# Two halves counted apart, and row indices made at arrival, in the routed-expert stage of a transformer layer kernel

## The chip, the cores and the metric

The kernel runs on one core of a Trainium2 chip. Its time is the device time of one execution in microseconds, taken as the median of several runs. TensorE (PE) does the matrix products; VectorE (DVE) and ScalarE (ACT) do elementwise work and copy out of PSUM; GpSimd (POOL) issues the indirect DMAs; SyncE (SP) and ACT issue the direct ones. All engines work beside each other and order themselves by semaphores. A DMA adds 16 to its semaphore when it has landed.

## The reference

x has 64 sequences of 64 tokens with 256 features, 4096 tokens in all. The reference adds two things to it.

```python
x = x + attention1(moe8_top2(x))             # 8 experts, 2 of them a token, and a shared one
x = x + ffn(attention2(x))                   # layernorm, shared key and value, causal, layernorm
# ffn: xf (4096 x 256)
tidx, tw = route(xf)                         # 64 experts, 8 a token, weights normed and scaled by 2.5
for e in experts:                            # up_w[e]: 256 x 128, down_w[e]: 128 x 256
    acc += combine[:, e, None] * (relu(xf @ up_w[e]) ** 2 @ down_w[e])
out = acc + shared(xf)
```

The change touches the loop over the 64 routed experts and nothing else.

## The kernel before

Ahead of the last stage the kernel has written, for each pair of a token and one of its 8 experts, a row of 258 numbers into a DRAM table `x_slots`: the token's 256 features, a number from which the pair's row in the result table is made (entry D), and the routing weight (entry D + 1). The table is sorted by expert and padded to blocks of 128 slots with one expert each: 320 blocks. Slots that hold no pair get an index past the end, and a scatter leaves them out.

The last stage is `slot_experts` (L1827). It takes the blocks in 80 groups of four (`GB = 4`). A group's work is spread over three turns of a software pipeline, and the five engines each run the same sequence of turns (`pipeline`, L1870): turn n does step 0 of group n, step 1 of group n - 1 and step 2 of group n - 2. `w` is n modulo 4.

- Step 0. SP loads the group's 512 slot rows to `xs` (L1900), in one of two buffers, as soon as DVE's `t_dve` tells that the group two before has been copied. PE transposes them (L1934) once the rows have landed and ACT and DVE have copied the transposes of the group before. ACT copies half of the transposes to `xsT` (L1981), DVE the other half (L2031); ahead of it DVE copies index number and weight of each row to `tail` (L2030), a ring of four (`TR`). ACT also copies the four experts' up weights to `up` (L1978).
- Step 1. PE makes z, the up products (L1945); ACT makes relu(z) (L1986) and DVE multiplies it by max(z, 0) into `hT` (L2036).
- Step 2. PE makes y, the down products of the four blocks (L1957), in two PSUM banks, 4 and 5. One count, `y_ps`, tells that all four are there. ACT scales blocks 0 and 1 by the routing weight into `ys` (L1992), DVE makes the row indices `yidx` from `tail` (L2044) and scales blocks 2 and 3 (L2047). Then POOL, after waiting for both, issues four indirect DMAs (L1914), one a block, that scatter the rows of `ys` to the DRAM table `y_rows`, a row for each pair.

`ys` and `yidx` have two buffers. So ACT and DVE wait, ahead of step 2, until the scatters of the group two before have landed; one semaphore of each buffer counts all four (`y_out[w % 2]`). In a turn, each engine does step 0 first, then step 1, then step 2, in the order of the program. PE waits for both ACT's and DVE's outputs of the group before ahead of its y products.

From turn 28 on (`HOLD`) there is a fourth kind of work. A tile of 128 tokens has all of its rows in `y_rows` by then. In each turn ACT issues the gather of half a tile's rows (512 KB, L2005), after its step 2, and DVE adds them up in three additions (L2056, L2060, L2065) at the end of the next turn. ACT stores a finished tile to `out` every second turn. Ahead of a tile's first gather ACT waits until all scatters up to some groups back have landed. After group 79 the rest of the 64 halves is gathered and added with nothing beside it.

Nothing in this stage is ordered by a planner: the order of the instructions on each engine is that of the code in `turn`.

Of the kernel before, what the change touches and what calls it, by code (L numbers as in the profile page):

```python
# [15 lines left out]
P = 128  # L16
# [29 lines left out]
GB = 4  # L46
# [67 lines left out]
def build(nc, x, xT, condT, cond, bias2, mask, w1gate, w1up, w1down, wtT, wgT,  # L114
# [3 lines left out]
    with ctx:  # L118
# [1708 lines left out]
        def slot_experts():  # L1827
# [4 lines left out]
            with ph:  # L1832
# [3 lines left out]
                def sem(name):  # L1836
# [23 lines left out]
                t_ps, t_act, t_dve, up_ready, z_ps, r_ready, h_ready, y_ps, y_act, y_dve = (  # L1860
                    sem(n) for n in ("t_ps", "t_act", "t_dve", "up_ready", "z_ps", "r_ready", "h_ready",
                                     "y_ps", "y_act", "y_dve"))
                block = ph.enter_context(nc.Block())
                LAG = 2

# [39 lines left out]
                @block.gpsimd  # L1905
                def _(pool):
                    def turn(n, w, q, live, u):
                        if live(2):
                            g = n - 2
                            pool.wait_ge(y_act, g + 1)  # L1910
                            pool.wait_ge(y_dve, g + 1)
                            pool.nop(nofuse=True)
                            for b in range(GB):
                                pool.indirect_dma_start(  # L1914
                                    out=y_rows, out_offset=bass.IndirectOffsetOnAxis(ap=yidx[:, w % 2, b:b + 1], axis=0),
                                    in_=ys[:, w % 2, b, :], in_offset=None,
                                    bounds_check=T * K2 - 1, oob_is_err=False).then_inc(y_out[w % 2], 16)
                    pipeline(pool, turn)
                    for w in range(2):
                        pool.wait_ge(y_out[w], NG // 2 * 16 * GB)  # L1920

                @block.tensor
                def _(pe):
# [3 lines left out]
                    def turn(n, w, q, live, u):  # L1927
# [20 lines left out]
                        if live(2):  # L1948
                            g = n - 2
                            e = experts_of(pe, regs, g)  # L1950
                            pe.wait_ge(h_ready, g + 1)
                            if isinstance(g, int) and g == 0:
                                pe.wait_ge(wd_in, (-(-EARLY // WCOLS) - (EARLY - E2) // WCOLS) * 16)
                            wait(pe, y_act, g)
                            wait(pe, y_dve, g)
                            for b in range(GB):
                                last = pe.matmul(ps[:, 4 + b // 2, (b % 2) * D:(b % 2 + 1) * D],  # L1957
                                                 hT[:, w % 2, b, :],
                                                 w_dn[:, bass.ds(e[b], 1), :].rearrange("p o n -> p (o n)"),
                                                 start=True, stop=True)  # L1960
                            last.then_inc(y_ps, 1)
                    pipeline(pe, turn)

                @block.scalar
                def _(act):
# [6 lines left out]
                    def turn(n, w, q, live, u):  # L1972
# [9 lines left out]
                        if live(1):  # L1982
                            g = n - 1
                            act.wait_ge(z_ps, g + 1)
                            wait(act, y_ps, g - 1)
                            act.activation(hT[:, (w - 1) % 2].rearrange("p b m -> p (b m)"), ps[:, 2, :], ACT.Relu).then_inc(r_ready, 1)  # L1986
                        if live(2):
                            g = n - 2
                            act.wait_ge(y_ps, g + 1)
                            wait(act, y_out[w % 2], half(q, w, 2) * 16 * GB)  # L1990
                            for b in range(2):
                                last = act.activation(ys[:, w % 2, b, :], ps[:, 4, b * D:(b + 1) * D], ACT.Copy,  # L1992
                                                      scale=tail[:, (w - 2) % TR, b, 1:2])
                            last.then_inc(y_act, 1)
                        if u is not None and not (isinstance(u, int) and u >= HALVES):
                            act.nop(nofuse=True)
                            tile = q * 2 + w // 2 - HOLD // 2
                            if w == 0:
                                done = q * 2 - 2 if not isinstance(q, int) else min(q * 2 - 2, NG // 2)
                                for sent in y_out:  # L2000
                                    act.wait_ge(sent, done * 16 * GB)
# [20 lines left out]
                def _(dve):  # L2022
                    def turn(n, w, q, live, u):
                        if live(0):
                            dve.wait_ge(t_ps, n + 1)
                            wait(dve, z_ps, n - 1)
                            wait(dve, y_act, n - TR + 1)
                            wait(dve, y_dve, n - TR + 1)
                            dve.nop(nofuse=True)
                            dve.tensor_copy(tail[:, w], xs[:, w % XR, :, D:D + 2])  # L2030
                            dve.tensor_copy(xsT[:, w % 2, 2:4].rearrange("p b c m -> p (b c m)"), ps[:, 1, :]  # L2031
                                            ).then_inc(t_dve, 1)
                        if live(1):
# [4 lines left out]
                                                     ).then_inc(h_ready, 1)  # L2038
                        if live(2):
                            g = n - 2  # L2040
                            dve.wait_ge(y_ps, g + 1)
                            wait(dve, y_out[w % 2], half(q, w, 2) * 16 * GB)

                            dve.tensor_scalar(yidx[:, w % 2, :], tail[:, (w - 2) % TR, :, 0], -1.0, float(T * K2),  # L2044
                                              ALU.mult, ALU.add)
                            for b in range(2, GB):
                                last = dve.tensor_scalar(ys[:, w % 2, b, :], ps[:, 5, (b - 2) * D:(b - 1) * D],  # L2047
                                                         tail[:, (w - 2) % TR, b, 1:2], None, ALU.mult)
# [100 lines left out]
```

## Time and profile before

| | us |
|---|---|
| median of 3 runs | 1892.97 |
| lowest and highest | 1887.82, 1893.12 |
| the profiled execution | 1889.07 |
| its span, first to last instruction | 1887.3 |
| POOL's scatters of this stage (L1914) | 323.3 busy, 320 of them |
| gathers of a half tile (L2005) | 64, 5.0 to landing |

The profile is of one execution. Its page gives each engine's busy time, the span in 40 slices, the chain of work that ended last followed back from the end, and groups of instructions. Times of single instructions come from the trace of the same execution, and are counted from the span's start. The stage of the change lies between some 1384 us, when its first slot rows are on their way, and the end. A POOL row of a scatter shows the time in which POOL makes the transfer's descriptors, not the transfer. Busy PE time is modelled at its end.

### The profile page before, as it was taken

Reading aid. Unit: us, or ns where it says so; the run is one execution under the profiler, and the core shown is the slowest. Engines: PE = TensorE matmul, PEld = TensorE weight load, DVE = VectorE, ACT = ScalarE, POOL = GpSimd, SP = SyncE. Lnnn points to the kernel's source line nnn. Section 1 sums busy time; section 2 is a strip of 40 time slices with the busy share of each in tenths; the row PEclk is TensorE's granted clock in tenths of the full one; section 3 lists DMA queues with packets and bytes.
Section 4 is the critical chain, followed back from the end, with each engine's and each line's share of the span. In section 5 each row is a group of like instructions: output and inputs, shape, how many; then the busy total and the mean of one; then the engine's idle time right before and its main releaser. Section 6 shows DMA issues by size and latency. Waiting matters only on the chain. (4 is left out here: it accounts for less than half of the span.)

```text
span 1887.3 us, 35739 instructions
## 1 busy us (share of the span) xinstructions
PE 1552.3 (82%) x12092; PEld 1241.4 (66%) x12093; DVE 1238.6 (66%) x3320; ACT 824.3 (44%) x1581; POOL 1000.5 (53%) x869
## 2 busy tenths in 40 slices
PE   5699999988888869989998898987039888888880
PEld 2588888854655547777776777755038886777770
DVE  2677776746767655688878888797214446666674
ACT  2233333223444434555555555544025555555550
POOL 1233333336665432226565566667717776766772
PEclk9899999999998989999999999998559999999996
DMA  5278458012000000001111111117646678988975
GB/s 151 64 187 230 116 137 232 1 31 57 24 24 13 13 23 2 1 1 57 57 49 55 57 55 59 49 63 280 189 175 191 194 208 271 284 280 260 280 218 166
DMA packets 155436, 226.61 MB, mean 120 GB/s; under 512 B 28840, under 2 KB 127791, under 8 KB 153140
## 3 DMA queue, kind: packets, MB, share of 16 engines
q1 hardware_dynamic: 113124, 115.37, 21.9%
q0 software_dynamic: 27648, 67.44, 10.1%
q10 hardware_dynamic: 14544, 42.21, 7.0%
q8 instruction: 75, 1.23, 0.3%
q14 instruction: 45, 0.37, 0.1%
HBM read 110.57 MB, written 122.75 MB: 124 GB/s over the span
## 5 line engine op out<-in xcount | busy, mean ns | idle before, releaser
L1914 POOL DMA_INDIRECT y_rows<-se_ys,se_yidx x320 | 323.3, 1010 | 158.3 <-issue 96.6
L1106 POOL DMA_INDIRECT x_slots<-wide,a_sidx x256 | 251.2, 981 | 71.6 <-issue 71.1
L442 POOL TENSOR_TENSOR e_hl<-e_h,e_hh 128x512 fp32r<-128x512 f32 x80 | 103.6, 1295 | 228.9 <-ACT e_hh L426 228.9
L1095 POOL TENSOR_TENSOR flat<-flat,a_rs 128x512 f32<-128x512 f32 x64 | 67.4, 1053 | 234.2 <-DVE a_rs L1582 234.2
L1957 PE MATMUL ps<-wide,se_hT 128*128 x640 | 157.4, 389 | 26.6 <-DVE se_ys L2047 26.2
L1934 PE MATMUL ps<-ident,se_xs 128*128 128x128 f32 x640 | 89.2, 285 | 101.4 <-DMA se_xs<-x_slots 80.1
L1945 PE MATMUL ps<-se_xsT,se_up 128*128 128x128 f32 x1280 | 163.0, 281 | 5.4 <-DVE se_hT L2036 3.9
L1945 PEld LDWEIGHTS ps<-se_xsT,se_up 128*128 128x128 f32 x1280 | 152.4, 195 | 13.6 <-issue 8.1
L1934 PEld LDWEIGHTS ps<-ident,se_xs 128*128 128x128 f32 x640 | 75.1, 147 | 123.2 <-issue 81.4
L1978 ACT COPY se_up<-w_up 128x256 f32 x320 | 105.8, 402 | 99.8 <-issue 86.4
L1957 PEld LDWEIGHTS ps<-wide,se_hT 128*128 128x128 f32 x640 | 116.6, 192 | 46.3 <-issue 33.3
L374 PE MATMUL ps<-xh,wh 128*128 128x512 f32 x320 | 126.7, 396 | 15.2 <-PEq L189 15.2
L461 DVE SCALAR_TENSOR_TENSOR acc<-ps,e_cexp,acc 128x256 f32<-128x256 f32 x320 | 132.2, 476 | 1.0 <-PE ps L376 0.6
L1992 ACT ACTIVATE se_ys<-ps,se_tail 128x256 f32<-128x256 f32 x160 | 67.2, 471 | 139.4 <-DMA y_rows<-se_ys,se_yidx 132.6
L1216 PE MATMUL ps<-w_up 128*128 128x256 f32 x448 | 114.5, 404 | 14.5 <-DVE flat L1675 8.8
L375 PE MATMUL ps<-xl,wh 128*128 128x512 f32 x320 | 126.4, 395 | 0.0
L1176 PE MATMUL ps<-w_up,flat 128*128 128x256 f32 x512 | 120.2, 389 | 6.8 <-ACT flat L1352 6.8
L376 PE MATMUL ps<-xh,wl 128*128 128x512 f32 x320 | 125.4, 392 | 0.0
L469 DVE TENSOR_TENSOR e_r<-ps,e_r 128x512 f32<-128x512 f32 x80 | 55.3, 692 | 98.5 <-ACT e_r L423 98.5
L1176 PEld LDWEIGHTS ps<-w_up,flat 128*128 128x128 f32 x512 | 98.8, 195 | 29.2 <-ACT flat L1352 9.5
L579 POOL TENSOR_TENSOR flat<-flat,a_mx 128x1024 f32<-128x1024 f32 x32 | 60.9, 1903 | 93.2 <-DVE a_mx L801 93.2
L2036 DVE SCALAR_TENSOR_TENSOR se_hT<-ps,se_hT 128x512 f32<-128x512 f32 x80 | 55.3, 692 | 81.9 <-ACT se_hT L1986 81.3
(277 smaller groups left out, 3812.9 us busy)
## 6 DMA issues: line engine op xcount, KB each, us to landing
x_slots<-wide SPq DMA_DIRECT2D x40, 1032.0 KB, 14.4
se_xs<-x_slots SPq DMA_DIRECT2D x80, 516.0 KB
se_got<-y_rows ACTq DMA_DIRECT2D x64, 512.0 KB, 5.0
w_up<-in_up SPq DMA_DIRECT2D x8, 1024.0 KB, 16.9
y_rows<-se_ys,se_yidx POOLq DMA_INDIRECT x320
wide<-in_xT SPq DMA_DIRECT2D x2, 2048.0 KB, 10.3
flat<-in_x SPq DMA_DIRECT2D x8, 512.0 KB, 3.9
x_slots<-wide,a_sidx POOLq DMA_INDIRECT x256, 2.9
```

What stands on the lines that cost most here:

```text
L374: pe.matmul(out, h0, h1, start=start, stop=False)
L375: pe.matmul(out, h0, l1, start=False, stop=False)
L376: return pe.matmul(out, l0, h1, start=False, stop=stop)
L461: last = dve.scalar_tensor_tensor(acc[:, tile, :], y_bank(n, t), cexp[:, w, tile:tile + 1], acc[:, tile, :], ALU.mult, ALU.add)
L1106: pool.indirect_dma_start(out=x_slots, out_offset=bass.IndirectOffsetOnAxis(ap=sidx[:, t, k_:k_ + 1], axis=0), in_=stage[:, t, k_, :], in_ ...
L1176: last = pe.matmul(ps[:, 1, 0:D], oT[:, j, :], wo[:, j, :], start=(j == 0), stop=(j == J2 - 1))
L1216: last = pe.matmul(bank[:, a * 2 * P:(a + 1) * 2 * P], wq[:, c, (2 * jj + a) * P:(2 * jj + a + 1) * P], xT_[:, c, u * 2 * P:(u + 1) * 2 * ...
L1914: pool.indirect_dma_start(out=y_rows, out_offset=bass.IndirectOffsetOnAxis(ap=yidx[:, w % 2, b:b + 1], axis=0), in_=ys[:, w % 2, b, :], in ...
L1934: last = pe.transpose(ps[:, b // 2, (b % 2 * C + c) * P:(b % 2 * C + c + 1) * P], xs[:, w % XR, b, c * P:(c + 1) * P], ident[:])
L1945: last = pe.matmul(ps[:, 2, b * P:(b + 1) * P], up[:, (w - 1) % 2, b, c, :], xsT[:, (w - 1) % 2, b, c, :], start=(c == 0), stop=(c == C - 1))
L1957: last = pe.matmul(ps[:, 4 + b // 2, (b % 2) * D:(b % 2 + 1) * D], hT[:, w % 2, b, :], w_dn[:, bass.ds(e[b], 1), :].rearrange("p o n -> p ...
L1978: last = act.copy(up[:, w % 2, b], w_up[:, bass.ds(e[b], 1)].rearrange("p o c m -> p (o c) m"))
```

## The change

Step 2's two halves get counts of their own. `y_ps` becomes `ya_ps` (blocks 0 and 1, PSUM bank 4, ACT) and `yb_ps` (blocks 2 and 3, bank 5, DVE). `y_out` gets one semaphore for each buffer and half. PE waits for ACT's half of the group before ahead of its first two products, and for DVE's ahead of the other two. POOL issues the first half's scatters after `y_act` alone, then waits for `y_dve` and issues the others. ACT, ahead of its half, waits for the first half's scatters of the group two before; DVE for the second half's.

`yidx` becomes a ring of four and is made in step 0, straight from `xs`, ahead of the copies to `tail` and `xsT`; `tail` now holds the weight alone. As POOL's scatters read the indices, DVE waits in step 0 of turn n until both halves of group n - 4 have landed. POOL waits for `t_dve` too, which tells that the indices are there.

```diff
-                yidx = sb("yidx", [P, 2, GB], I32)
-                tail = sb("tail", [P, TR, GB, 2])
+                yidx = sb("yidx", [P, TR, GB], I32)
+                tail = sb("tail", [P, TR, GB])
...
-                y_out = [sem("y_out0"), sem("y_out1")]
+                y_out = [[sem("y_out0a"), sem("y_out0b")], [sem("y_out1a"), sem("y_out1b")]]
...
 # POOL, step 2
-                            pool.wait_ge(y_act, g + 1)
-                            pool.wait_ge(y_dve, g + 1)
-                            pool.nop(nofuse=True)
-                            for b in range(GB):
-                                pool.indirect_dma_start(
-                                    out=y_rows, out_offset=bass.IndirectOffsetOnAxis(ap=yidx[:, w % 2, b:b + 1], axis=0),
-                                    in_=ys[:, w % 2, b, :], in_offset=None,
-                                    bounds_check=T * K2 - 1, oob_is_err=False).then_inc(y_out[w % 2], 16)
+                            pool.wait_ge(t_dve, g + 1)
+                            for side, done in enumerate((y_act, y_dve)):
+                                pool.wait_ge(done, g + 1)
+                                pool.nop(nofuse=True)
+                                for b in range(2 * side, 2 * side + 2):
+                                    pool.indirect_dma_start(
+                                        out=y_rows,
+                                        out_offset=bass.IndirectOffsetOnAxis(ap=yidx[:, (w - 2) % TR, b:b + 1], axis=0),
+                                        in_=ys[:, w % 2, b, :], in_offset=None,
+                                        bounds_check=T * K2 - 1, oob_is_err=False).then_inc(y_out[w % 2][side], 16)
...
 # PE, step 2
-                            wait(pe, y_act, g)
-                            wait(pe, y_dve, g)
-                            for b in range(GB):
-                                last = pe.matmul(ps[:, 4 + b // 2, (b % 2) * D:(b % 2 + 1) * D],
...
-                            last.then_inc(y_ps, 1)
+                            for side, (free_, full) in enumerate(((y_act, ya_ps), (y_dve, yb_ps))):
+                                wait(pe, free_, g)
+                                for b in range(2 * side, 2 * side + 2):
+                                    last = pe.matmul(ps[:, 4 + side, (b % 2) * D:(b % 2 + 1) * D],
...
+                                last.then_inc(full, 1)
...
 # ACT, step 1, then step 2
-                            wait(act, y_ps, g - 1)
+                            wait(act, yb_ps, g - 1)
...
-                            act.wait_ge(y_ps, g + 1)
-                            wait(act, y_out[w % 2], half(q, w, 2) * 16 * GB)
+                            act.wait_ge(ya_ps, g + 1)
+                            wait(act, y_out[w % 2][0], half(q, w, 2) * 32)
...
 # DVE, step 0
+                            wait(dve, y_out[w % 2][0], half(q, w, 2) * 32)
+                            wait(dve, y_out[w % 2][1], half(q, w, 2) * 32)
                             dve.nop(nofuse=True)
-                            dve.tensor_copy(tail[:, w], xs[:, w % XR, :, D:D + 2])
+                            dve.tensor_scalar(yidx[:, w, :], xs[:, w % XR, :, D], -1.0, float(T * K2), ALU.mult, ALU.add)
+                            dve.tensor_copy(tail[:, w, :], xs[:, w % XR, :, D + 1])
                             dve.tensor_copy(xsT[:, w % 2, 2:4].rearrange("p b c m -> p (b c m)"), ps[:, 1, :]
                                             ).then_inc(t_dve, 1)
...
 # DVE, step 2
-                            dve.wait_ge(y_ps, g + 1)
-                            wait(dve, y_out[w % 2], half(q, w, 2) * 16 * GB)
-
-                            dve.tensor_scalar(yidx[:, w % 2, :], tail[:, (w - 2) % TR, :, 0], -1.0, float(T * K2),
-                                              ALU.mult, ALU.add)
+                            dve.wait_ge(yb_ps, g + 1)
+                            wait(dve, y_out[w % 2][1], half(q, w, 2) * 32)
+                            dve.nop(nofuse=True)
```

ACT's wait ahead of a tile's first gather goes over the four semaphores in place of two, with the same groups in it.

## Rows read from the trace of the kernel before

**Rows 1.** The page's slices: busy tenths of the DMA engines, 40 equal parts.
```profile
DMA  5278458012000000001111111117646678988975
```
**Rows 2.** The page's chain that ended last, share of the span.
```profile
DMA y_rows<-se_ys,se_yidx 7%; POOL y_rows L1914 5%; DMA se_got<-y_rows 1%; PE ps L1945 1%; DVE se_ys L2047 1%; PE ps L1957 1%; DMA se_xs<-x_slots 1%; PE ps L1934 1%; ACT se_up L1978 0%; ACT se_hT L1986 0%; DVE se_yidx L2044 0%; POOLq L1914 0%; DVE se_got L2056 0%; ACT se_xsT L1981 0%; ACTq L1867 0%
```
**Rows 3.** Busy by stretch: length, busy (count), PEclk, DMA share, GB/s; L1914, then all engines.
```profile
1411.80:1552.00 140.20, 105.21 (x107) 0.99 0.63 192
1552.00:1832.00 280.00, 197.92 (x194) 0.98 0.87 270
...
1552.00:1838.00 286.00, 243.75 (x1585) 207.39 (x1583) 187.81 (x450) 156.97 (x400) 202.68 (x199) 0.98 0.86 267
```
**Rows 4.** Waits after 1360 us: total, times, longest.
```profile
ACT se_ys L1992 <- DMA y_rows<-se_ys,se_yidx: 132.6, 68, 5.5
...
DVE se_yidx L2044 <- DMA y_rows<-se_ys,se_yidx: 84.1, 57, 4.7
...
PE ps L1934 <- DMA se_xs<-x_slots: 80.1, 7, 73.6
```
**Rows 5.** The chain in order of time: start, length; from a last scatter's start to landing.
```profile
1443.07 3.95 DMA y_rows<-se_ys,se_yidx
...
1515.51 5.45 DMA y_rows<-se_ys,se_yidx
...
1662.16 5.59 DMA y_rows<-se_ys,se_yidx
...
1673.67 5.80 DMA y_rows<-se_ys,se_yidx
```
**Rows 6.** POOL's scatters in order of time: start, length, idle time before.
```profile
1669.62 1.16 POOL L1914 DMA_INDIRECT y_rows<-se_ys,se_yidx  x1 [0.82 <-DVE se_ys L2047]
1671.09 0.99 POOL L1914 DMA_INDIRECT y_rows<-se_ys,se_yidx  x1 [0.30 <-issue]
...
1673.67 0.99 POOL L1914 DMA_INDIRECT y_rows<-se_ys,se_yidx  x1 [0.30 <-issue]
```
**Rows 7.** DVE in order of time.
```profile
1667.85 0.17 DVE L2044 TENSOR_SCALAR se_yidx<-se_tail 128x4 int32<-128x4 f32 x1 [0.58 <-DMA y_rows<-se_ys,se_yidx]
1667.93 0.87 DVE L2047 TENSOR_SCALAR se_ys<-ps,se_tail 128x256 f32<-128x256 f32 x2
...
1811.64 0.68 DVE L2031 COPY se_xsT<-ps 128x512 f32<-128x512 f32 x1
1812.63 0.69 DVE L2036 SCALAR_TENSOR_TENSOR se_hT<-ps,se_hT 128x512 f32<-128x512 f32 x1 [0.31 <-ACT se_hT L1986]
```
**Rows 8.** PE in order of time.
```profile
1677.76 1.06 PE L1934 MATMUL ps<-ident,se_xs 128*128 128x128 f32 x8 [1.38 <-DMA se_xs<-x_slots]
...
1691.12 1.94 PE L1934 MATMUL ps<-ident,se_xs 128*128 128x128 f32 x8 [2.91 <-DMA se_xs<-x_slots]
...
1812.47 1.06 PE L1934 MATMUL ps<-ident,se_xs 128*128 128x128 f32 x8 [0.34 <-DVE se_xsT L2031]
1813.47 2.02 PE L1945 MATMUL ps<-se_xsT,se_up 128*128 128x128 f32 x16
1815.33 1.89 PE L1957 MATMUL ps<-wide,se_hT 128*128 x8
1817.11 1.09 PE L1934 MATMUL ps<-ident,se_xs 128*128 128x128 f32 x8
```
**Rows 9.** DVE's copies that let the rows of 1677.76 and 1691.12 be loaded.
```profile
1670.54 0.69 DVE L2031 COPY se_xsT<-ps 128x512 f32<-128x512 f32 x1
...
1682.60 0.68 DVE L2031 COPY se_xsT<-ps 128x512 f32<-128x512 f32 x1
```
**Rows 10.** ACT after a landing, its gather's issue, and gathers on the page.
```profile
1802.25 0.84 ACT L1992 ACTIVATE se_ys<-ps,se_tail 128x256 f32<-128x256 f32 x2 [0.93 <-DMA y_rows<-se_ys,se_yidx]
1802.70 0.34 ACTq L2005 DMA_DIRECT2D se_got<-y_rows  x1
...
se_got<-y_rows ACTq DMA_DIRECT2D x64, 512.0 KB, 5.0
```

More of the change, by code:

```diff
@@ L1909, in turn @@
                             g = n - 2
-                            pool.wait_ge(y_act, g + 1)
-                            pool.wait_ge(y_dve, g + 1)
-                            pool.nop(nofuse=True)
-                            for b in range(GB):
-                                pool.indirect_dma_start(
-                                    out=y_rows, out_offset=bass.IndirectOffsetOnAxis(ap=yidx[:, w % 2, b:b + 1], axis=0),
-                                    in_=ys[:, w % 2, b, :], in_offset=None,
-                                    bounds_check=T * K2 - 1, oob_is_err=False).then_inc(y_out[w % 2], 16)
+                            pool.wait_ge(t_dve, g + 1)
[8 more added lines that the diff above has]
+                                        bounds_check=T * K2 - 1, oob_is_err=False).then_inc(y_out[w % 2][side], 16)
                     pipeline(pool, turn)
                     for w in range(2):
-                        pool.wait_ge(y_out[w], NG // 2 * 16 * GB)
+                        for side in range(2):
+                            pool.wait_ge(y_out[w][side], NG // 2 * 32)
                 @block.tensor
@@ L1953, in turn @@
                                 pe.wait_ge(wd_in, (-(-EARLY // WCOLS) - (EARLY - E2) // WCOLS) * 16)
-                            wait(pe, y_act, g)
-                            wait(pe, y_dve, g)
-                            for b in range(GB):
-                                last = pe.matmul(ps[:, 4 + b // 2, (b % 2) * D:(b % 2 + 1) * D],
-                                                 hT[:, w % 2, b, :],
-                                                 w_dn[:, bass.ds(e[b], 1), :].rearrange("p o n -> p (o n)"),
-                                                 start=True, stop=True)
-                            last.then_inc(y_ps, 1)
+                            for side, (free_, full) in enumerate(((y_act, ya_ps), (y_dve, yb_ps))):
+                                wait(pe, free_, g)
+                                for b in range(2 * side, 2 * side + 2):
+                                    last = pe.matmul(ps[:, 4 + side, (b % 2) * D:(b % 2 + 1) * D],
+                                                     hT[:, w % 2, b, :],
+                                                     w_dn[:, bass.ds(e[b], 1), :].rearrange("p o n -> p (o n)"),
+                                                     start=True, stop=True)
+                                last.then_inc(full, 1)
                     pipeline(pe, turn)
@@ L1988, in turn @@
                             g = n - 2
-                            act.wait_ge(y_ps, g + 1)
-                            wait(act, y_out[w % 2], half(q, w, 2) * 16 * GB)
+                            act.wait_ge(ya_ps, g + 1)
+                            wait(act, y_out[w % 2][0], half(q, w, 2) * 32)
                             for b in range(2):
                                 last = act.activation(ys[:, w % 2, b, :], ps[:, 4, b * D:(b + 1) * D], ACT.Copy,
-                                                      scale=tail[:, (w - 2) % TR, b, 1:2])
+                                                      scale=tail[:, (w - 2) % TR, b:b + 1])
                             last.then_inc(y_act, 1)
@@ L1999, in turn @@
                                 done = q * 2 - 2 if not isinstance(q, int) else min(q * 2 - 2, NG // 2)
-                                for sent in y_out:
-                                    act.wait_ge(sent, done * 16 * GB)
+                                for sent in y_out[0] + y_out[1]:
+                                    act.wait_ge(sent, done * 32)
                                     act.nop(nofuse=True)
@@ L2040, in turn @@
                             g = n - 2
[L2041 to L2045 removed]
+                            dve.wait_ge(yb_ps, g + 1)
+                            wait(dve, y_out[w % 2][1], half(q, w, 2) * 32)
+                            dve.nop(nofuse=True)
                             for b in range(2, GB):
                                 last = dve.tensor_scalar(ys[:, w % 2, b, :], ps[:, 5, (b - 2) * D:(b - 1) * D],
[L2048 removed]
+                                                         tail[:, (w - 2) % TR, b:b + 1], None, ALU.mult)
                             last.then_inc(y_dve, 1)
```

4 lines of the change are left out of this document (2 added, 2 removed).

## Prediction

> **What bounds the kernel now.** I read the page's slices first, then the chain of waits, then POOL's scatters by stretch, then single turns. The last stage runs from slice 30 on, and the DMA engines stand at 7 to 9 tenths in it [rows 1]; in its longest stretch POOL is busy 197.92 of 280 us and DVE 187.81 of 286 [rows 3], so neither is plainly full. The chain's longest piece is the landing of the y scatters, then their issue on POOL [rows 2]. So the stage hangs on POOL and on what POOL waits for.
>
> Rows 3 split it. Between 1411.8 and 1552 us POOL issues 107 scatters in 140.2 us: 1.31 us each. Back to back one takes 1.29 us (0.99 plus a pause of 0.30: 1671.09 [rows 6]), so there POOL is full: 5.17 us for a group of four. Between 1552 and 1832, with the gathers running, 194 scatters take 280 us: 1.443 each, 5.77 a group. At 1.29 they would take 250.3 us. What can be won in that stretch is at most 29.7 us, and about 2 in the first.
>
> Why 5.77: ACT and DVE wait for the landing of the group two before, because one count holds all four scatters of a buffer; they wait 132.6 and 84.1 us [rows 4]. One ring of two groups: last scatter issued to landing 5.7 us (5.59, 5.80 [rows 5]); indices 0.08 (1667.85 to 1667.93) and both products 0.87 [rows 7]; 0.82 until POOL starts (1668.80 to 1669.62); first to last scatter 4.05 (1669.62 to 1673.67 [rows 6]). Sum 11.52, 5.76 a group: the measured 5.77. In the first stretch landing took 3.95 [rows 5]: 9.8 for two, under POOL's 10.34, and POOL rules.
>
> **The change, part by part.** Work is nearly unchanged: the same 4 products, 4 scatters, one index operation of 0.17 and one tail copy (half as wide) per group. Cost 0; DVE is idle a third of the stretch [rows 3]. POOL gets one wait and one nop more. Where POOL is late, its first scatter takes 1.16, not 0.99 [rows 6]. If both halves are late, that is 0.17 x 48.5 groups = 8 us; if not, 0, as a group's border costs nothing when POOL isn't late. I take 0: the second half has the 2.6 us of the first half's scatters as cover.
>
> *Halves apart.* ACT's half is free when the first two scatters of the old group have landed, 2 x 1.29 = 2.6 us before the last. It needs only the first half of the product. The old ring shrinks: ACT's side no longer waits for the last landing. For DVE's side the ring ends with two scatters, not four: 5.7 + DVE's work + 0.82 + 1.29.
>
> *Indices at arrival.* This is where something is added. DVE now waits at the head of turn n for both halves of group n-4 (the ring of four index slots), before the indices, the tail and the copy of xT(n). The same landing was awaited before, at the turn's end, behind xT(n) and hT(n-1). Behind the waiting instruction now stand: xT(n), which lets SP load the slot rows of n+2 and PE transpose n+1; hT(n-1), which lets PE run product z(n); DVE's half of y(n-2); and the gather's additions. From landing: 0.08 for the indices, as much for the tail, 0.68 for xT: 0.84 to its end (1811.64), hT 0.69, y 0.87 [rows 7]: 2.4 to 2.6 before POOL can have the second half. New rings:
> - DVE's half, 2 groups: 5.7 + 2.5 + 0.82 + 1.29 = 10.3, 5.16 a group: level with POOL.
> - Through the transposes, 3 groups: 5.7 + 0.84 + 0.15 to PE (1812.32 to 1812.47) + transposes 1.00 + z 1.86 + half a y product 1.0 [rows 8] + ACT's half 0.9 (0.84 [rows 10] and a hand-over) + 0.82 + 4.05 = 16.3, 5.44 a group.
> - Through the load of slot rows, 4 groups: landing n-4, xT(n), load of n+2, transposes, z(n+1), y(n), scatters of n: 5.7 + 0.84 + X + 3.86 + 0.9 + 0.82 + 4.05 = 16.17 + X. X is DVE's copy to the rows' arrival. No row gives it as such. Below: 1817.11 minus 1812.32, 4.8 us, no wait for rows. Above: 1677.76 minus 1671.23, 6.5, and 1691.12 minus 1683.28, 7.8, where PE did wait [rows 8, 9]; beside the first, of 73.6 us, there were six such waits in the stage, 6.5 us together [rows 4]. X = 4.8, 6.5, 7.8 give 5.24, 5.67, 5.99 a group. I take 6.0, nearer to 6.5 since the rows' load is then bunched behind the landing: 22.2 / 4 = 5.54.
>
> Second stretch: the longest ring, 5.54, 0.23 below 5.77, times 48.5 groups: -11 us (at X = 4.8 the three-group ring takes over, 5.44 and -16; at X = 7.8 it is +11). First stretch: with 3.95 to 5.45 landing [rows 5], say 4.5, the rings are 15.1 / 3 = 5.03 and (14.97 + 6.0) / 4 = 5.24 against POOL's 5.17: 0, at most +2, at best -2. The start gains under 1 us, as POOL may begin with ACT's half. The tail of gathers alone after the last scatter is untouched, and for the few scatters after 1832 I count nothing.
>
> Sum: span 1887.3 - 11 = 1876; the profiled execution took 1889.07 beside that span, so 1878; the median of the runs shown, 1892.97, stands 3.9 above it: 1882.
>
> **A rule weighed.** The row shows a DMA share of 0.87 in the gathering stretch, 0.63 before it, and landings of 3.95 in the one and 5.8 in the other [rows 3, 5]. The Trainium skill, page "DMA: Bandwidth & Descriptors", section "Queues, rings and completion order", says that each DMA engine takes turns between the queues that have work for it. By it a load that starts together with a gather would get half the engines' turns; the trace's longer landings agree. This is the third rival's mechanism.
>
> **The rivals.** A difference under 0.3% (5.7 us) is what a measurement here can't tell from none.
> 1. POOL full throughout (chance 0.12): landing and X stay short, everything hides behind 1.29 x 4. 28 to 30 us less: 1864. For: POOL and both landings were level in the first stretch. Against: the three-group ring of 5.44, and the DMA share would go to 0.87 x 5.77 / 5.17 = 0.97.
> 2. One wait replaces the other (0.25): X near 6.9 gives 23.1 / 4 = 5.77; or the share goes up and landings with it (by 5.77 / 5.54 x 0.87 = 0.91 for my forecast). 0 to -4: 1891. For: 6.5 was seen with the load spread out. Against: 4.8 was seen too, in the same stretch.
> 3. Slower (0.18): the load of slot rows and the gather meet. Now ACT sends the gather 0.45 us after the landing (1802.70, the landing at 1802.25) and the load goes 3.4 us after it (1667.85 to 1671.23 [rows 7, 9]); both carry some 512 KB, and a gather takes 5.0 us [rows 10]. By my ring the load goes 0.84 after the landing; ACT's half of n ends 0.84 + 6.0 + 3.86 + 0.9 = 11.6 after it, so that of n-2, ahead of the gather in turn n, ends 11.6 - 2 x 5.54 = 0.5 after it: both leave within 0.4 us. If X passes 6.9, the turn is longer than before; at 7.4 it is 23.57 / 4 = 5.89, +6 us, and the first stretch, where X is not hidden any more either, adds up to +2: 1899 to 1901. For: 7.8 was seen once. Against: the scatters between them are spread better, and gathers tolerate a late landing (DVE takes them 2.3 us or more after).
> That the change doesn't do what it says I rule out: the counts and the waits are plain in the diff.
>
> **How the numbers follow.** Forecast 0.45 (5.45 to 5.65 a group, -15 to -6: 1878 to 1887), rivals 0.12, 0.25, 0.18. Faster by over 0.3% (under 1887.3): rival 1 and nearly all of the forecast, 0.12 + 0.43 = 0.55. Within: 0.02 of the forecast and 0.24 of rival 2, 0.26. Slower (over 1898.6): rival 3 and 0.01 of rival 2, for POOL's 0.17 us restarts, 0.19. The range holds the forecast, rival 2, most of rival 3's lower end and rival 1's upper: 1866 to 1899.
>
> **What would show it.** In the profile after: ACT's waits for y_rows nearly gone, replaced by waits for PE's y product; DVE's wait for y_rows standing before the index operation at the head of the turn, in the size of 80 us or more; PE's transposes waiting for se_xs and for DVE's copy, tens of us instead of the 6.5 for rows; 194 scatters in about 269 us of the gathering stretch. If POOL shows no pauses beyond 0.30, rival 1 holds; if the transposes wait over 1 us for rows in most turns, rival 2 or 3. Wrong would be: a first stretch longer by more than 3 us, or ACT still waiting for landings.

## The result, and the profile after

The changed kernel took 1905.32 us (median of 20 runs, 1888.38 to 1912.65) against 1892.95 for the one before (20 runs, 1887.82 to 1900.34): ratio 1.0066, 95% interval 1.0051 to 1.0081. The forecast was 1882 and faster; it is slower, by 12.4 us. The profiled execution took 1911.96 us, near the top of its range, with a span of 1910.2 (before: 1889.07 and 1887.3), so the trace shows nearly twice the loss of the medians: 22.9 us against 12.4.

POOL's scatters by stretch, as in [rows 3]: length, busy (count), granted clock, DMA share, GB/s; changed kernel.

```profile
1411.80:1552.00 140.20, 106.41 (x108) 1.00 0.64 192
1552.00:1832.00 280.00, 177.97 (x178) 0.89 0.82 254
```

The first stretch is as it was (108 scatters, 107 before). In the gathering stretch there are 178 in 280 us in place of 194: 6.29 us a group in place of 5.77. That is nearly the whole loss (the last scatter starts at 1879.20 us in place of 1857.01), and the granted clock there went from 0.98 to 0.89. Who waited, as in [rows 4]: total, times, longest.

```profile
PE ps L1937 <- DMA se_xs<-x_slots: 81.5, 6, 73.6
PE ps L1937 <- DVE se_xsT L2037: 68.6, 34, 4.2
...
DVE se_yidx L2035 <- DMA y_rows<-se_ys,se_yidx: 128.8, 45, 5.0
...
ACT se_ys L1995 <- PE ps L1960: 22.2, 66, 1.4
ACT se_ys L1995 <- DMA y_rows<-se_ys,se_yidx: 2.6, 1, 2.6
```

ACT's 132.6 us of waiting for landings are down to 2.6, as the change meant. DVE's went from 84.1 to 128.8, at the head of the turn, and behind them PE's transposes wait 68.6 us for DVE's copy (6.2 before). For slot rows PE waits 7.9 us beside the first wait, in five turns that all lie between 1584 and 1616 us: the load that I feared binds there and nowhere after.

One round of the ring, in order of time: start, length, idle time before. It is the three-group ring of the prediction.

```profile
1691.09 0.17 DVE L2035 TENSOR_SCALAR se_yidx<-se_xs 128x4 int32<-128x4 f32 x1 [4.98 <-DMA y_rows<-se_ys,se_yidx]
...
1691.24 0.68 DVE L2037 COPY se_xsT<-ps 128x512 f32<-128x512 f32 x1
...
1692.07 1.94 PE L1937 MATMUL ps<-ident,se_xs 128*128 128x128 f32 x8 [4.24 <-DVE se_xsT L2037]
...
1693.80 3.55 PE L1948 MATMUL ps<-se_xsT,se_up 128*128 128x128 f32 x16
...
1697.19 1.89 PE L1960 MATMUL ps<-wide,se_hT 128*128 x8
...
1698.35 0.84 ACT L1995 ACTIVATE se_ys<-ps,se_tail 128x256 f32<-128x256 f32 x2 [0.28 <-PE ps L1960]
...
1700.03 0.98 POOL L1915 DMA_INDIRECT y_rows<-se_ys,se_yidx  x1 [3.44 <-issue]
...
1703.89 0.98 POOL L1915 DMA_INDIRECT y_rows<-se_ys,se_yidx  x1 [0.30 <-issue]
...
1710.58 0.17 DVE L2035 TENSOR_SCALAR se_yidx<-se_xs 128x4 int32<-128x4 f32 x1 [4.32 <-DMA y_rows<-se_ys,se_yidx]
```

Landing seen to DVE's copy done 0.83, to PE 0.15, start of the transposes to start of y 5.12, to ACT 1.16, ACT 0.84, to POOL 0.84, first to last scatter 3.86, to the landing 6.69: 19.49 us for three groups. The forecast for the same steps was 16.3. Two terms make the difference: transposes and z take 5.12 in place of 2.86 (+2.26), and the landing 6.69 in place of 5.7 (+0.99). The first comes with the clock. After PE has stood 4.24 us the transposes take 1.94 us and z 3.55; in the next turn they take 1.04 and 1.95. After a shorter pause the clock holds:

```profile
1590.58 1.06 PE L1937 MATMUL ps<-ident,se_xs 128*128 128x128 f32 x8 [1.92 <-DVE se_xsT L2037]
1591.48 1.95 PE L1948 MATMUL ps<-se_xsT,se_up 128*128 128x128 f32 x16
1593.27 1.89 PE L1960 MATMUL ps<-wide,se_hT 128*128 x8
```

The length of the pause alone doesn't decide it. After pauses of 3.88 and 4.02 us (1767.50 and 1805.01) the transposes still ran at full speed and only the z products behind them were slow:

```profile
1767.50 1.06 PE L1937 MATMUL ps<-ident,se_xs 128*128 128x128 f32 x8 [3.88 <-DVE se_xsT L2037]
1768.40 3.21 PE L1948 MATMUL ps<-se_xsT,se_up 128*128 128x128 f32 x16
```

The granted clock in the round shown, behind the pause and in the turn after it (length, busy of PE, PEld, DVE, ACT and POOL, then clock, DMA share, GB/s):

```profile
1692.10:1696.90 4.80, 4.80 (x23) 4.80 (x24) 3.53 (x9) 0.59 (x1) 2.47 (x3) 0.50 0.60 180
1698.90:1703.30 4.40, 4.40 (x33) 4.14 (x32) 3.50 (x9) 2.91 (x9) 2.67 (x3) 1.00 0.81 270
```

This round is one of the longer ones. From DVE's wait at 1632.70 to that at 1839.19 the ring goes round eleven times without a break, in 18.77 us on the mean: 4.52 from the start of the transposes to the start of y (3.87 to 5.15), and landings of 6.46. Against the forecast's 2.86 and 5.7 that is 1.66 us for the first and 0.76 for the second.

So the ring lengthens itself: waiting for one landing in three turns, PE falls to the lower of its two clocks (0.50 of full speed, 1.2 GHz), and comes late to the next. The Trainium skill, page "TensorE: Matmul & The Clock Gate", section "Part 1: The HAM clock gate", says that a monitor lets the array run at full or at half clock by how busy PE has been of late. The rows agree: 1.94 over 1.04 and 3.55 over 1.95 are 1.87 and 1.82, near a factor of two.

### The profile page after: what moved, and what is told of

It is laid out like the page before. It is cut to its first block and busy times, and to the rows that moved or that the text cites. A ratio compares the mean times of both kernels' runs of the same rounds, so it can differ in the third digit from the quotient of the medians.

```text
span 1910.2 us, 35964 instructions
## 1 busy us (share of the span) xinstructions
PE 1556.2 (81%) x12092; PEld 1262.7 (66%) x12093; DVE 1236.7 (65%) x3320; ACT 831.2 (44%) x1581; POOL 994.9 (52%) x869
## 5 line engine op out<-in xcount | busy, mean ns | idle before, releaser
L1915 POOL DMA_INDIRECT y_rows<-se_ys,se_yidx x320 | 318.7, 996 | 185.5 <-issue 136.1
L1937 PE MATMUL ps<-ident,se_xs 128*128 128x128 f32 x640 | 96.1, 300 | 150.5 <-DMA se_xs<-x_slots 81.5
L1937 PEld LDWEIGHTS ps<-ident,se_xs 128*128 128x128 f32 x640 | 80.5, 155 | 170.6 <-issue 167.5
L1948 PE MATMUL ps<-se_xsT,se_up 128*128 128x128 f32 x1280 | 177.2, 299 | 0.2 <-DVE se_hT L2042 0.2
L1948 PEld LDWEIGHTS ps<-se_xsT,se_up 128*128 128x128 f32 x1280 | 171.2, 216 | 0.6 <-issue 0.4
L1960 PE MATMUL ps<-wide,se_hT 128*128 x640 | 153.4, 384 | 0.3 <-ACT se_ys L1995 0.3
L2035 DVE TENSOR_SCALAR se_yidx<-se_xs 128x4 int32<-128x4 f32 x80 | 18.0, 225 | 209.5 <-DMA y_rows<-se_ys,se_yidx 128.8
L1216 PEld LDWEIGHTS ps<-w_up 128*128 128x128 f32 x448 | 85.2, 198 | 34.2 <-DVE flat L1675 11.2
```

The source lines that it names most:

```text
L1216: last = pe.matmul(bank[:, a * 2 * P:(a + 1) * 2 * P], wq[:, c, (2 * jj + a) * P:(2 * jj + a + 1) * P], xT_[:, c, u * 2 * P:(u + 1) * 2 * ...
L1915: pool.indirect_dma_start(out=y_rows, out_offset=bass.IndirectOffsetOnAxis(ap=yidx[:, (w - 2) % TR, b:b + 1], axis=0), in_=ys[:, w % 2, b, ...
L1937: last = pe.transpose(ps[:, b // 2, (b % 2 * C + c) * P:(b % 2 * C + c + 1) * P], xs[:, w % XR, b, c * P:(c + 1) * P], ident[:])
L1948: last = pe.matmul(ps[:, 2, b * P:(b + 1) * P], up[:, (w - 1) % 2, b, c, :], xsT[:, (w - 1) % 2, b, c, :], start=(c == 0), stop=(c == C - 1))
L1960: last = pe.matmul(ps[:, 4 + side, (b % 2) * D:(b % 2 + 1) * D], hT[:, w % 2, b, :], w_dn[:, bass.ds(e[b], 1), :].rearrange("p o n -> p (o ...
```

## The experiments

Ten kernels ran, some of them several times, in five groups and eighteen runs. In the first and the last group the kernel before took 1893 us. In the three between it took 2035 to 2052 us, once on the very chip of the first group, and the ratios of those three are compared with each other alone.

### 1 and 2. Each part by itself

Halves apart alone (e1_halves_only): the changed kernel, with

```diff
 # POOL, step 2
-                            pool.wait_ge(t_dve, g + 1)
+                            pool.wait_ge(idx_ready, g + 1)
...
 # DVE, step 0
-                            wait(dve, y_out[w % 2][0], half(q, w, 2) * 32)
-                            wait(dve, y_out[w % 2][1], half(q, w, 2) * 32)
...
-                            dve.tensor_scalar(yidx[:, w, :], xs[:, w % XR, :, D], ...)
...
 # DVE, step 2, from a two-column tail, ring of four
+                            wait(dve, y_out[w % 2][0], (half(q, w, 2) - 1) * 32)
+                            wait(dve, y_out[w % 2][1], (half(q, w, 2) - 1) * 32)
...
+                            dve.tensor_scalar(yidx[:, (w - 2) % TR, :], tail[:, (w - 2) % TR, :, 0], ...).then_inc(idx_ready, 1)
```

> The changed kernel with one part undone: row indices are made in step 2 again (from a two-column tail, in a ring of four, with a count of their own), so VectorE no longer waits for a landing at the head of its turn; the two halves stay apart. Theory A (the wait at the head, in the ring landing - VectorE's copy - transposes - z - y - scatters, is what makes the change slow): that ring is gone, POOL goes from 6.3 us a group to 5.2 to 5.5 in the gathering stretch, the granted clock there is back at 0.97 or more, and the kernel beats the one before: 1865 to 1885. Theory B (the halves apart are what is slow: POOL waits twice, the scatters come in longer clumps and land later): it stays above the one before, 1898 to 1910, with landings of 6.5 us and more.

Measured: 1886.35 us, ratio 0.9965 (0.9948 to 0.9983).

Indices at arrival alone (e2_early_only): the kernel before, with

```diff
+                            wait(dve, y_out[w % 2], half(q, w, 2) * 16 * GB)   # step 0
...
+                            dve.tensor_scalar(yidx[:, w, :], xs[:, w % XR, :, D], ...)
...
-                            dve.tensor_scalar(yidx[:, w % 2, :], tail[:, (w - 2) % TR, :, 0], ...)   # step 2
```

> The kernel before with the other part alone: indices made at arrival in a ring of four, with VectorE's wait for the landing of group n-4 at the head of turn n; the four scatters of a group and both products still counted together. Theory A: now both the head wait and the old ring stand: VectorE's half comes 2.5 us after a landing in place of 0.95, before all four scatters, 5.7 + 2.5 + 0.8 + 4.05 = 13.1 for two groups, 6.5 a group against 5.77: slower than before by 30 to 45 us, 1922 to 1940. Theory B: about the time of before, 1888 to 1898.

Measured: 1944.09 us, ratio 1.0276 (1.0259 to 1.0293). POOL's scatters by stretch in e2:

```profile
1411.80:1552.00 140.20, 98.67 (x101) 1.00 0.58 174
1552.00:1832.00 280.00, 173.61 (x171) 0.93 0.79 244
```

and DVE's wait for landings in it:

```profile
DVE se_yidx L2031 <- DMA y_rows<-se_ys,se_yidx: 203.5, 68, 4.7
```

171 scatters in 280 us are 6.55 us a group; 6.5 was written down. DVE's waits for landings are 203.5 us. The wait at the head of the turn is what costs: 2.76% on top of the old ring, and 1.0% on top of the halves (1.0066 against 0.9965). The halves are what pays: theory B falls. The sizes of e1 were missed by theory A all the same. The halves alone gain 0.35%, not the 0.4% to 1.5% that were expected, and the gathering stretch runs at the old pace. POOL's scatters in the stretch, in e1:

```profile
1552.00:1832.00 280.00, 193.01 (x194) 0.92 0.85 267
```

PE's waits for slot rows in e1:

```profile
PE ps L1938 <- DMA se_xs<-x_slots: 114.0, 23, 73.2
```

One of them, behind DVE's copy that released its load, in order of time:

```profile
1675.27 0.68 DVE L2035 COPY se_xsT<-ps 128x512 f32<-128x512 f32 x1
...
1684.94 1.94 PE L1938 MATMUL ps<-ident,se_xs 128*128 128x128 f32 x8 [2.83 <-DMA se_xs<-x_slots]
```

PE now waits for slot rows, 40.8 us in 22 turns. PE's transposes at 1684.94 came 9.0 us after the copy that released their rows' load (1675.95), and 5.8 to 9.3 us after it in the 22 turns, where the prediction allowed 4.8 to 7.8. And in those pauses the clock falls here too (1.94, and 0.92 for the stretch). A part of what the halves take away is replaced by this wait for loads. ACT still waits 34.9 us for landings in e1, and POOL 9.0 us in 27 turns for the indices, which the first half's scatters need too.

### 3. Idle products for the clock, too many

```diff
+                            for b in range(8 if u is not None else 0):
+                                pe.matmul(ps[:, 3, 0:P], ident[:], ident[:], start=True, stop=True)
                             pe.wait_ge(x_in[w % XR], (q * 2 + w // 2 + 1) * 16)
```

> The changed kernel with eight products of the identity with itself (about 1.0 us, into a PSUM bank that nothing reads) ahead of PE's waits for its transposes, in the gathering turns alone. In the changed kernel's trace PE stands still for 2.5 to 4.2 us in every third turn and comes back with transposes of 1.94 in place of 1.04 us and z products of 3.55 in place of 1.95. Theory A1 (PE's clock falls in these pauses and adds 2.3 us to the ring of three groups, 19.5 us): the pause shrinks, the granted clock in the gathering stretch goes from 0.89 to 0.97 or more, the ring to about 17.2, 5.75 a group, and the kernel loses 10 to 25 us: 1882 to 1895. Theory A2 (the ring is slow for the later landings, 6.7 in place of 5.7 us, and the clock is only a bystander): 1.0 us of work more changes nothing or costs, 1903 to 1912.

> The kernel before with the same eight idle products in the gathering turns: the control. Its PE is granted 0.98 already and has about 4.7 us of work in 5.77. Theory A1 and A2 both: no gain; 0 to +10 us, 1892 to 1903, as PE comes near to being full. A gain of over 6 us would say that the fill helps by something other than the clock's fall in the pauses of the changed kernel.

Measured: 1910.94 us, 1.0100 (1.0086 to 1.0114), on the changed kernel, and 1909.64, 1.0101 (1.0083 to 1.0119), on the one before. All engines in the gathering stretch (PE, PEld, DVE, ACT, POOL, clock, DMA share, GB/s), first the changed kernel:

```profile
1552.00:1832.00 280.00, 280.00 (x2175) 270.52 (x2174) 175.49 (x411) 150.65 (x363) 178.34 (x181) 1.00 0.81 257
```

and the one before:

```profile
1552.00:1832.00 280.00, 280.00 (x2183) 270.86 (x2182) 174.80 (x411) 147.66 (x364) 186.77 (x183) 1.00 0.86 258
```

PE is full in both, so both go at PE's pace. The 1911 us lie in the range of theory A2, and the control is 7 us above its own, but by this fill and not by the ring. I had put eight products at 1.0 us; four take 0.89, from their start to the transposes behind them in h1, below, so eight take 1.8. The pair tells nothing of what the clock costs. PE in h1 (four products, L1933), in order of time:

```profile
1628.10 1.05 PE L1933 MATMUL ps<-ident 128*128 128x128 f32 x8
1628.99 1.04 PE L1939 MATMUL ps<-ident,se_xs 128*128 128x128 f32 x8
```

### 4. Four idle products, and a quarter of the gathers

The loop of 3 with 4 in place of 8, and for the gathers

```diff
-                            act.dma_start(got[:, w % 2], yv[...][:, w % 2]).then_inc(here[w % 2], 16)
+                            act.dma_start(got[:, w % 2, 0:1], yv[...][:, w % 2, 0:1]).then_inc(here[w % 2], 16)
...
+                    dve.memset(got[:], 0.0)     # once, ahead of DVE's turns
```

In the last group, where before took 1892.83 and the changed kernel itself was not run:

> The changed kernel with four idle products ahead of the transposes in the gathering turns, where before takes 1893 us if this call meets that state. Theory A1 (the clock's fall in PE's pauses lengthens the ring: transposes to y product take 4.1 to 5.2 us there and 2.7 at the full clock): 0.994 to 1.002 of before. Theory A2 (bystander): 1.005 or more.

> The changed kernel that gathers one of four parts (its routed sum lacks three quarters). Theory A (the gathers' transfers make landings late and so the ring long): landing under 5 us, POOL at 5.2 to 5.4 a group in the gathering stretch, 0.975 to 0.985 of before. Theory C (the additions and issues beside them do it): 1.000 or more.

Measured: h1 1897.02 us, 1.0015 (0.9995 to 1.0035); h2 1870.15 us, 0.9870 (0.9848 to 0.9891). POOL's stretch in h1:

```profile
1552.00:1832.00 280.00, 191.18 (x191) 0.99 0.86 266
```

and in h2:

```profile
1552.00:1832.00 280.00, 199.82 (x199) 0.95 0.70 205
```

In h1 the clock is granted at 0.99, and 191 scatters go through in place of 178: 5.86 us a group. PE has 0.9 us more to do in each turn and the kernel is faster than the changed one, 1.0015 against 1.0066, the intervals apart. The landings are as late as in the changed kernel. In one turn of h1, in order of time, DVE sees one 7.76 us after its last scatter's start, and PE goes on at full speed:

```profile
1768.56 0.98 POOL L1915 DMA_INDIRECT y_rows<-se_ys,se_yidx  x1 [0.30 <-issue]
...
1776.32 0.17 DVE L2037 TENSOR_SCALAR se_yidx<-se_xs 128x4 int32<-128x4 f32 x1 [4.69 <-DMA y_rows<-se_ys,se_yidx]
...
1777.30 1.06 PE L1939 MATMUL ps<-ident,se_xs 128*128 128x128 f32 x8 [1.22 <-DVE se_xsT L2039]
1778.20 1.95 PE L1950 MATMUL ps<-se_xsT,se_up 128*128 128x128 f32 x16
```

In the stretch's turns with over 2 us of waiting at the head, the landing takes 6.40 us on the mean in h1 (19 turns) and 6.38 in the changed kernel (17); from the transposes' start to y's it is 2.66 to 2.69 us in all 19 of h1, and 4.05 on the mean of the 17. So the clock is a cause, not a bystander. By the ratios it carries some 0.51 of the 0.66 points, 10 us of 12; with both intervals, 0.26 to 0.76. What four idle products cost by themselves in this condition wasn't measured: the kernel before with four ran only among the runs of section 5. The transposes of h1 then wait for slot rows, 14.2 us in 18 turns (87.3 with the first, of 73.1), as in e1.

In h2 POOL reaches 5.63 us a group, short of the 5.2 to 5.4 written down. Landings, counted as above, take 5.28 us on the mean of 16 turns and 6.73 at most, not under 5. The transfers of the gathers do make the stretch long: from 1.0066 to 0.9870 are 37 us, of which 9 lie in the shorter tail (31.0 us from the last scatter's start to the end in the changed kernel, 21.7 in h2), and some 28 ahead of it. The kernel before wasn't run with a quarter of the gathers. It may gain as much, so h2 doesn't say how much of the loss between the two kernels is the gathers' doing. Theory C falls, as the additions are all there; the ratio is just over theory A's 0.985. In the same profile the clock stands at 0.95, so less is lost to it too, and the two effects aren't told apart in h2.

### 5. The three groups in between

In the traces of these groups ACT and DVE stop, 2.6 to 3.7 us on the mean of a trace and 7.7 at the longest, at places where no engine of the core releases them; the kernel before with four idle products has these stops too. The traces of the first and the last group have none. Waits in the changed kernel (f1), of which those on `remote` are stops:

```profile
ACT se_hT L1989 <- remote: 118.2, 36, 7.6
...
DVE se_yidx L2035 <- DMA y_rows<-se_ys,se_yidx: 35.8, 14, 5.2
```

What the stops are stays open. With them the order of the kernels is another.

First of the three (before: 2050.69 us):

> The changed kernel with four idle products ahead of PE's transposes in the gathering turns, in place of eight. Eight filled PE wholly (280.00 busy of 280, in the changed kernel and in the one before alike, 1911 and 1910 us), so they told nothing of the clock; one costs 0.22 us, and four bring PE to 4.4 + 0.9 = 5.3 us a group, under the changed kernel's 6.3. Theory A1 (the clock's fall in PE's pauses adds 2.3 us to a ring of 19.5): granted clock 0.97 or more in the gathering stretch, 5.7 to 5.9 a group, 1885 to 1897 us, at least 8 us under the changed kernel. Theory A2 (the clock is a bystander, the late landings set the ring): 1903 to 1912.

> Control: the kernel before with the same four idle products. Its granted clock is 0.98 there. Theory A1 and A2 both: 1888 to 1898, within 0.3% of before.

> The changed kernel, which gathers only the first of the four parts of each half tile (128 KB in place of 512 KB); the buffer is cleared once ahead and all additions stay, so the routed sum lacks three quarters. All instructions of the engines are the same. Theory A (the ring from the landing through VectorE's copy to the scatters is long because the gathers make landings and row loads late): landing falls from 6.7 to under 5 us, the ring to 14.5 to 15.5 for three groups, POOL is full at 5.2 a group in the gathering stretch, and the time is 1855 to 1875. Theory C (the DVE and ACT work that comes with the gathers, additions and issues, is what delays the head of the turn): the stretch stays near 6 a group, over 1890.

> The halves apart alone (the first experiment, 1886), and SP's load of the next slot rows released by VectorE's copy of the tail, no longer by its copy of the transposes, 0.7 us earlier (a count of its own). In the first experiment PE waited 41 us in 22 turns for slot rows, 8.2 us after the copy at the worst, against 6.5 us in 6 before. Theory D (with the landing's ring gone the load of slot rows is the next limit): PE's waits for se_xs fall to 25 us or less and the kernel gains 5 to 15 us more, 1872 to 1882. Theory E (the DMA engines' share as a whole is the limit, and what is issued earlier arrives no earlier): within 3 us of 1886.

The edit of e6, on top of e1:

```diff
-                            wait(sp, t_dve, n - XR + 1)
+                            wait(sp, x_free, n - XR + 1)     # x_free counts DVE's copies to tail
```

Second (before: 2052.14):

> The changed kernel itself, so that the three beside it can be read against it: on the chip of the last four runs the kernel before took 2051 us and not 1893, and the changed one was not among them. Every theory: the ratio to before of the first timing, 1.005 to 1.008, on a chip where before takes 1893.

> The changed kernel with four idle products ahead of PE's transposes in the gathering turns, now beside the changed kernel itself. Theory A1 (the clock's fall in PE's pauses adds 2.3 us to a ring of 19.5): granted clock 0.97 or more in the gathering stretch, 5.7 to 5.9 a group, 8 to 20 us under the changed kernel of this call. Theory A2 (bystander): within 4 us of it.

> The changed kernel that gathers one of four parts (its routed sum lacks three quarters), now beside the changed kernel. Theory A (gathers make landings and row loads late, and so the ring long): landings under 5 us, POOL near 5.2 a group in the gathering stretch, 30 to 50 us under the changed kernel. Theory C (the additions and issues on DVE and ACT do it): within 10 us of it.

> Halves apart alone with the early release of the load, 0.992 of before on the slower chip. Theory D (the load of slot rows is the next limit): 0.990 to 0.993 of before, 1874 to 1880 where before takes 1893, PE's waits for se_xs at 25 us or less. Theory E (the DMA share is the limit): 0.996 to 0.998, as without the early release.

Third (before: 2034.54):

> The changed kernel with four idle products in the gathering turns, once more: in the two calls in which it ran the kernel before took 2051 us, with stops of 4 to 5 us on ACT and DVE that no engine releases, and the changed kernel itself stood at 0.9935 of before there, so they say nothing of the state in which before takes 1893 and the changed one 1.0066 of it. Theory A1 (the clock's fall in PE's pauses adds 2.3 us to a ring of 19.5): ratio to before 0.994 to 1.002. Theory A2 (bystander): 1.005 or more.

> The changed kernel that gathers one of four parts (its routed sum lacks three quarters). Theory A (the gathers make landings late and so the ring long): landing under 5 us, POOL near 5.2 a group in the gathering stretch, 0.975 to 0.985 of before. Theory C (additions and issues on DVE and ACT do it): 1.000 or more.

> Halves apart alone with the early release of the slot rows' load. Theory D (the load is the next limit): 0.990 to 0.993 of before. Theory E (the DMA share is): 0.996 to 0.998, as without the early release (0.9965).

> The same with three idle products ahead of the transposes in the gathering turns. In the halves-only kernel the granted clock in the gathering stretch was 0.92, so pauses of PE bring the clock down there too. If the clock matters there (A1): 2 to 8 us under the kernel without the fill. If not (A2): the same or up to 5 us over.

| kernel | ratio to before, first, second, third |
|---|---|
| the changed one (f1) | -, 0.9935, - |
| before, four idle products (e4) | 1.0037, -, - |
| changed, four idle products (e4, f2, g1) | 0.9966, 0.9961, 1.0003 |
| changed, a quarter of the gathers (e5, f3, g2) | 0.9898, 0.9874, 0.9900 |
| halves, early load (e6, f4, g3) | 0.9924, 0.9921, 0.9953 |
| the same, three idle products (g4) | -, -, 0.9978 |

Under the stops the change gains 0.65% (0.9911 to 0.9959) instead of losing 0.66%. DVE's waits for landings are 35.8 us in place of 128.8. That fits an account in which the scatters have mostly landed when DVE comes to the head of the turn, and the halves' gain is left; no run tests it. Idle products cost 0.25 points where the partner ran in the same group (f2 against f1, within the intervals; g4 against g3), and 0.37 on the kernel before, so they give nothing back here: theory A1 was missed in f2 and g4. Why isn't shown. Theory A's ranges for a quarter of the gathers were missed in all three groups, f1 came out the other way than written down, and the control of e4 lies just over its 0.3%. A quarter of the gathers gives 0.6 points (f3 against f1) in place of 2.0. The 8.2 us that the expectation of e6 names as e1's worst load is too low: it is 9.3. So none of these runs tells theory A1 from A2, or D from E, for the condition in which the result was taken. There PE's waits for slot rows were e1's limit, and here they are nearly gone in all of them (2.8 us in f4, 11.4 in g3, none in e6). The early load was never run in the result's condition, and whether it adds to e1's gain is open.

## Why the prediction was wrong

- *What bounds the kernel.* Held: the gathering stretch is where the time changed, and the pace before follows from the ring of landing, products and four scatters. e2 gives that ring with DVE's 2.5 us put into it, and its 6.5 us a group came out as 6.55. Its time, 1944, was still 4 us above the range.
- *Halves apart.* Held in its mechanism: ACT's waits for landings went from 132.6 to 2.6 us, and e1 alone is faster by 0.35%. The 2.6 us owe something to the slower turn: at the old pace, in e1, ACT still waits 34.9 us.
- *POOL's extra wait and nop at 0.* Held where POOL isn't late: the first stretch has 108 scatters against 107. The cover that I gave the second half was thinner than thought: POOL waited for DVE's products 18 times, 12.0 us in all. It wasn't tested by itself.
- *First stretch at 0.* Held.
- *Through the transposes, 5.44 a group.* This is the step that failed. The ring is real and it binds, but it was sized at 16.3 us for three groups and measured 19.49 in the round shown (18.9 by the stretch's mean of 6.29 a group). PE's 1.00 and 1.86 us were taken from turns in which PE had hardly paused. I never asked what the pause that the ring puts before the transposes would do to them: 2.26 us of 3.2 in this round, 1.66 of some 2.4 on the mean of the eleven. The sign stood in [rows 8]: the transposes of 1691.12, behind a pause of 2.91, took 1.94 us. I used that row for the load's X alone. h1 shows that this is a cause. The landing, 5.7 at a given load of the DMA engines, was held fixed as well; it was 6.69 in this round, 0.99 of 3.2, and 6.46 on the mean of the eleven. Why landings grew is open: those that DVE waited for in the stretch took 5.2 us on the mean in the kernel before (36 of them) and 6.2 in the changed one (22), where the DMA share is lower, 0.82 against 0.87. Without the clock's term the eleven rounds would have taken 17.1 us each, 5.7 a group against 5.77 before. That is an estimate from these rows, and it leaves some 3 us of gain, not 11.
- *Through the load of slot rows, taken as the longest, 5.54 a group.* Wrong for the changed kernel: 7.9 us of waits for rows in 5 turns. It is the ring that appears once the head wait is gone (e1) or PE is kept busy (h1).
- *The rivals.* The time came out 4 us above rival 3's place, but not by its mechanism: the load and the gather may meet, PE hardly waits for the rows. Rival 3 put its point of decision at a load of 6.9 us; what decided was the three-group ring, with PE's clock as its largest term. The range's upper end, 1899, was that rival's, and no rival had the clock in it.
- *The signs to look for.* DVE's wait at the head, over 80 us, and PE's transposes waiting tens of us for DVE's copy were both there; the 269 us for 194 scatters were not (178 in 280 us, so some 305).

Working a ring out from rows gives its length only under the conditions of those rows. This forecast had 11 us of gain in it, from 0.23 us a group, less than either of the two terms moved (0.55 and 0.25 a group on the mean).

## What to carry to other kernels

A wait that is moved ahead of the copy that feeds the matmuls isn't the same wait: price what it does to TensorE's pauses, and where they grow long, take matmul durations from rows at the lower clock. When a ring of waits sets the pace, sum every ring that the change opens, in both clocks, and treat a win smaller than the clock's term as no forecast at all. In this kernel the early count (halves apart) is worth taking without the wait at the head: e1, at 1886.35 us and 0.9965 (0.9948 to 0.9983) of before, is faster than both kernels.

## What the runs showed of the hardware

- In the changed kernel a pause of PE before the transposes of 1.92 us was followed by full speed (1.06 us for eight of them), one of 4.24 us by transposes of 1.94 and z products of 3.55 in place of 1.04 and 1.95, and two of 3.88 and 4.02 us by transposes at full speed and z products of 3.2.
- Four idle products ahead of that pause (0.89 us of work) took the granted clock of the stretch from 0.89 to 0.99, with landings as late as without them (6.40 and 6.38 us).
- A load of 516 KB of slot rows, at a DMA share of 0.85, took 9.0 us from its release to PE's first transpose, and 5.8 to 9.3 in the 22 turns of e1 in which PE waited for it.
- In one condition, seen in three of the five groups of runs, the four kernels that ran in both took 7 to 9% longer, ACT and DVE stood for up to 7.7 us at a time, and the change's sign was the other one.
